# Two full transpositions in place of eight 64x64 products, for the per-head decays of a state-space layer

## The reference, cut to what matters

```
dt = softplus(dt + dt_bias)                # B, L, 64 heads
dA = exp(dt * (-exp(A_log)))
state = state * dA + (dt * x_t) B_t        # at each token, per head
y_t = state . C_t
```

## Time and profile before

| | |
|---|---|
| median of three runs | 776.09 us (773.34 to 778.7) |
| span of the profiled execution | 779.8 us |
| TensorE busy | 742.3 us (95%) |
| VectorE, ScalarE, GpSimd busy | 520.5, 492.4, 293.4 us |
| mean granted TensorE clock | 0.988 of full speed |
| one block in the middle of the mixer | 60 to 61 us |
| all eight-product turns, matmul records | 256, 11.6 us |
| make_dt, make_d, make_cum | 2.3, 2.3, 3.4 us in 8 blocks |
| step_decay, RUN, TO_END | 1.5, 2.4, 4.6 us in 8 blocks |

### The profile page before, as it was taken

The page is one execution under the profiler, slowest core; times in us unless marked ns, Lnnn a source line. Parts: engine busy times, 40 slices in busy tenths (PEclk is TensorE's granted clock), DMA queues, the critical chain, the costliest instruction groups (busy, mean ns, idle before and its releaser), DMA issues.

```text
span 779.8 us, 20312 instructions
## 1 busy us (share of the span) xinstructions
PE 742.3 (95%) x8486; PEld 609.8 (78%) x8486; DVE 520.5 (67%) x845; ACT 492.4 (63%) x933; POOL 293.4 (38%) x235
## 2 busy tenths in 40 slices
PE   4977999999999999999999998889999999999997
PEld 4855788888887887887887886568888888888886
DVE  6968976886887888797797796873633532632331
ACT  5989878978978977978879888533312321321330
POOL 2173275366456546627617707530010011001002
PEclk9988999999999999999999999999999999999999
DMA  9824243384485266266465378634113013003002
GB/s 297 228 69 109 44 105 111 92 241 127 82 236 142 79 158 211 88 148 201 139 158 184 83 202 316 200 99 160 41 55 108 0 37 125 0 13 95 0 1 84
DMA packets 42299, 94.97 MB, mean 122 GB/s; under 512 B 9888, under 2 KB 15776, under 8 KB 42016
## 3 DMA queue, kind: packets, MB, share of 16 engines
q1 hardware_dynamic: 42208, 93.67, 41.9%
HBM read 84.73 MB, written 17.57 MB: 131 GB/s over the span
## 4 chain that ended last, share of the span: by engine, by line
PE 60%; DVE 22%; ACT 10%; issue 5%; DMA 1%; POOL 1%; SPq 0%; DVEq 0%; ACTq 0%; POOLq 0%
PE ps_y L1684 10%; PE ps_proj L1671 9%; DVE cx L937 9%; PE ps_out L1671 6%; PE ps_x L1671 6%; PE ps_proj L1223 4%; PE ps_x L1272 4%; PE ps_proj L1224 3%; PE ps_proj L1225 3%; PE ps_y L1295 3%; DVE ring L992 3%; ACT ring L716 2%; DVE state L1002 2%; PE ps_x L1306 2%; DVE dt_p L912 2%
## 5 line engine op out<-in xcount | busy, mean ns | idle before, releaser
L531 POOL TENSOR_TENSOR ring<-tokd,ring 128x1024 f32<-128x1024 f32 x64 | 122.2, 1924 | 185.2 <-ACT tokd L711 127.5
L1223 PE MATMUL ps_proj<-xn_hi,win_x_hi 128*128 128x256 f32 x352 | 104.7, 298 | 1.7 <-DVE xn_lo L906 1.7
L1224 PE MATMUL ps_proj<-xn_lo,win_x_hi 128*128 128x256 f32 x352 | 100.2, 285 | 0.0
L1225 PE MATMUL ps_proj<-xn_hi,win_x_lo 128*128 128x256 f32 x352 | 100.0, 284 | 0.0
L937 DVE SCALAR_TENSOR_TENSOR cx<-cin,consts,cx 128x256 f32<-128x256 f32 x240 | 96.3, 475 | 0.0
L1540 POOL TENSOR_TENSOR res<-res,hidden 128x512 f32<-128x512 f32 (+1 forms) x16 | 20.1, 1256 | 166.3 <-DVE hidden L1603 165.3
L1223 PEld LDWEIGHTS ps_proj<-xn_hi,win_x_hi 128*128 128x128 f32 x352 | 67.7, 192 | 15.7 <-issue 14.0
L992 DVE TENSOR_TENSOR ring<-ring,ps_tok 128x1024 f32<-128x1024 f32 x64 | 75.6, 1214 | 4.8 <-ACT ring L720 4.7
L1223 PE MATMUL ps_proj<-xn_hi,win_z_hi 128*128 128x256 f32 x256 | 74.0, 289 | 0.0
L1224 PE MATMUL ps_proj<-xn_lo,win_z_hi 128*128 128x256 f32 x256 | 72.2, 282 | 0.0
L1225 PE MATMUL ps_proj<-xn_hi,win_z_lo 128*128 128x256 f32 x256 | 72.1, 282 | 0.0
(11 more groups left out here) (186 smaller groups left out, 1887.3 us busy)
## 6 DMA issues: line engine op xcount, KB each, us to landing
ring<-cum_dram SPq DMA_DIRECT2D x128, 256.0 KB, 4.8
xin<-x SPq DMA_DIRECT2D x8, 512.0 KB, 3.9
res<-x SPq DMA_DIRECT2D x32, 128.0 KB, 2.7
x_dram<-res SPq DMA_DIRECT2D x32, 128.0 KB, 2.9
res<-x_dram SPq DMA_DIRECT2D x16, 256.0 KB, 2.7
out<-res SPq DMA_DIRECT2D x15, 256.0 KB, 2.1
x_in_sb<-x_dram SPq DMA_DIRECT2D x3, 1024.0 KB, 5.6
gate_w_copy<-gate_w SPq DMA_DIRECT2D x4, 704.0 KB, 6.1
```

Source lines behind the costliest of these rows:

```text
L531: pool.tensor_tensor(ring[:, g, :, :], own, ring[:, g, :, :], ALU.subtract).then_inc(diffed, 1)
L1223: pe.matmul(out, hi[:, k, :], xn_hi[:, k, :], start=(k == 0), stop=False)
L1224: pe.matmul(out, hi[:, k, :], xn_lo[:, k, :], start=False, stop=False)
L1225: made = pe.matmul(out, lo[:, k, :], xn_hi[:, k, :], start=False, stop=(k == KT - 1))
```

## The change

`dts` goes. In its place are two tiles, each 128 partitions x 2 steps x 2 sequences x 64 tokens: `dt_cum` has DT of the 64 heads on partitions 0 to 63 (UPPER) and CUM on 64 to 127 (LOWER); `run_end` has RUN on UPPER and TO_END on LOWER. A step's 128 columns of each are turned by one 128x128 transposition. The result in PSUM, and all that reads it, is laid out as before. make_dt becomes two instructions, one a sequence, on 64 partitions each; make_d and the scan become one each on 64 partitions and 256 columns; RUN likewise; TO_END becomes four instructions a block (its bias is a column for one step and one sequence). One wait moves from the scan to make_d (the scan now works in place, so that make_d is the first to overwrite CUM); one wait of ScalarE goes, as dt_p is no longer read by the scan. `low_row`, a small row of the later test on the MLP's weights, moves into `low_buf`, whose readers are done by then.

```diff
-        dts = sb("dts", [P, 4, P])
+        dt_cum, run_end = sb("dt_cum", [P, STEPS, BATCH, Q]), sb("run_end", [P, STEPS, BATCH, Q])
+        UPPER, LOWER = slice(0, HEADS), slice(HEADS, P)
-        chain = sb("chain", [P, P])
+        chain = sb("chain", [P, STEPS * BATCH * Q])
...
-                    sp.dma_start(cum_dram[bass.ds(i, 1), j, :, :].rearrange("a r t -> (a r) t"),
-                                 dts[:, CUM, half(j)]).then_inc(cum_out, 16)
+                    sp.dma_start(cum_dram[i, j, :, :].rearrange("(b h) t -> h b t", b=BATCH),
+                                 dt_cum[LOWER, j, :, :]).then_inc(cum_out, 16)
...
-                    act.wait_ge(cum_made, j)
...
-                act.activation(step_decay[:], dts[:, CUM, Q - 1::Q], ACT.Exp).then_inc(step_decayed, 1)
+                act.activation(step_decay[:].rearrange("h b j -> h j b"), dt_cum[LOWER, :, :, Q - 1], ACT.Exp).then_inc(step_decayed, 1)
                 act.wait_ge(tokd_turned, STEPS * i)
-                act.activation(dts[:, RUN, :], dts[:, CUM, :], ACT.Exp).then_inc(run_made, 1)
+                act.activation(run_end[UPPER, :, :, :], dt_cum[LOWER, :, :, :], ACT.Exp).then_inc(run_made, 1)
                 for j in range(STEPS):
-                    at = (j + 1) * Q - 1
-                    made = act.activation(dts[:, TO_END, half(j)], dts[:, CUM, half(j)], ACT.Exp, scale=-1.0,
-                                          bias=dts[:, CUM, at:at + 1])
+                    for b in range(BATCH):
+                        made = act.activation(run_end[LOWER, j, b, :], dt_cum[LOWER, j, b, :], ACT.Exp, scale=-1.0,
+                                              bias=dt_cum[LOWER, j, b, Q - 1:Q])
...
-                dve.tensor_tensor(dts[:, DT, :], dt_v[:], dt_p[:], ALU.add).then_inc(dt_made, 1)
+                for b in range(BATCH):
+                    r = slice(b * HEADS, (b + 1) * HEADS)
+                    made = dve.tensor_tensor(dt_cum[UPPER, :, b, :], by_step(dt_v, r), by_step(dt_p, r), ALU.add)
+                made.then_inc(dt_made, 1)
...
-                dve.tensor_scalar(dt_p[:], dts[:, DT, :], neg_a[:], LOWEST, ALU.mult, ALU.max).then_inc(d_made, 1)
+                dve.tensor_scalar(dt_cum[LOWER, :, :, :], dt_cum[UPPER, :, :, :], neg_a[UPPER, :], LOWEST, ALU.mult, ALU.max).then_inc(d_made, 1)
...
-                dve.tensor_tensor_scan(dts[:, CUM, :], chain[:], dt_p[:], 0.0, ALU.mult, ALU.add).then_inc(cum_made, 1)
+                cums = dt_cum[LOWER, :, :, :].rearrange("p j b t -> p (j b t)")
+                dve.tensor_tensor_scan(cums, chain[LOWER, :], cums, 0.0, ALU.mult, ALU.add).then_inc(cum_made, 1)
...
-                for n in range(4):
-                    for b in range(BATCH):
-                        made = pe.matmul(ps_tokd[half(b), n * HEADS:(n + 1) * HEADS], dts[half(b), n, half(j)], eye[half(b), half(b)],
-                                         start=True, stop=True)
+                for n, pair in enumerate((dt_cum, run_end)):
+                    made = pe.transpose(ps_tokd[:, n * P:(n + 1) * P], pair[:, j, :, :].rearrange("p b t -> p (b t)"), eye[:])
                 made.then_inc(tokd_turned, 1)
```

More of the change, by code:

```diff
@@ L130, in __init__ @@
         self.low_buf = sb(ctx, "low_buf", [P, LOW_WIDTHS[2]])
-        self.low_row, self.low_any = sb(ctx, "low_row", [1, P]), sb(ctx, "low_any", [1, 1])
+        self.low_row, self.low_any = self.low_buf[0:1, 0:P], sb(ctx, "low_any", [1, 1])
         self.stats, self.moments = sb(ctx, "stats2", [P, TT, 6]), sb(ctx, "moments2", [P, TT, 2])
@@ L181, in mixer_phase @@
         dt_v, dt_e, dt_p = sb("dt_v", [P, P]), sb("dt_e", [P, P]), sb("dt_p", [P, P])
-        dts = sb("dts", [P, 4, P])
+        dt_cum, run_end = sb("dt_cum", [P, STEPS, BATCH, Q]), sb("run_end", [P, STEPS, BATCH, Q])
+        UPPER, LOWER = slice(0, HEADS), slice(HEADS, P)
         tok = sb("tok", [P, P])
         tokd = sb("tokd", [P, STEPS, 4, HEADS])
-        whole, step_decay = sb("whole", [P, BATCH * HEADS, STEPS]), sb("step_decay", [P, STEPS])
+        whole, step_decay = sb("whole", [P, BATCH * HEADS, STEPS]), sb("step_decay", [HEADS, BATCH, STEPS])
         consts = sb("consts", [P, C_N])
@@ L471, in _ @@
             sp.wait_ge(hand.low_all_made, 1)
-            sp.dma_start(hand.low_row[:], hand.low_all[:]).then_inc(hand.low_in, 16)
+            sp.dma_start(hand.low_row, hand.low_all[:]).then_inc(hand.low_in, 16)
             sp.dma_start(hand.scales[:], mlp_packed).then_inc(hand.scales_in, 16)
@@ L912, in soft, with by_step @@
                 dve.scalar_tensor_tensor(dt_p[:], dt_p[:], log_c[LOGN - 1 - n], dt_e[:], ALU.add, ALU.mult).then_inc(soft_step, 1)
+            def by_step(t, r):
+                return t[r, :].rearrange("p (j t) -> p j t", j=STEPS)
             def make_dt(j, opening=False):
@@ L917, in make_dt, with make_d, make_cum @@
                     dve.wait_ge(tokd_turned, STEPS * j)
-                dve.tensor_tensor(dts[:, DT, :], dt_v[:], dt_p[:], ALU.add).then_inc(dt_made, 1)
-            def make_d(j):
+                for b in range(BATCH):
+                    r = slice(b * HEADS, (b + 1) * HEADS)
+                    made = dve.tensor_tensor(dt_cum[UPPER, :, b, :], by_step(dt_v, r), by_step(dt_p, r), ALU.add)
+                made.then_inc(dt_made, 1)
+            def make_d(j, opening=False):
                 dve.wait_ge(dt_made, j + 1)
-                dve.tensor_scalar(dt_p[:], dts[:, DT, :], neg_a[:], LOWEST, ALU.mult, ALU.max).then_inc(d_made, 1)
-            def make_cum(j, opening=False):
-                dve.wait_ge(d_made, j + 1)
                 if not opening:
                     dve.wait_ge(cum_out, 32 * j)
-                dve.tensor_tensor_scan(dts[:, CUM, :], chain[:], dt_p[:], 0.0, ALU.mult, ALU.add).then_inc(cum_made, 1)
+                dve.tensor_scalar(dt_cum[LOWER, :, :, :], dt_cum[UPPER, :, :, :], neg_a[UPPER, :], LOWEST, ALU.mult, ALU.max).then_inc(d_made, 1)
+            def make_cum(j):
+                dve.wait_ge(d_made, j + 1)
+                cums = dt_cum[LOWER, :, :, :].rearrange("p j b t -> p (j b t)")
+                dve.tensor_tensor_scan(cums, chain[LOWER, :], cums, 0.0, ALU.mult, ALU.add).then_inc(cum_made, 1)
             def conv_tap(j, tiles, k):
@@ L1139, in any_low @@
                 dve.wait_ge(hand.low_in, 16)
-                dve.tensor_reduce(hand.low_any[:], hand.low_row[:], mybir.AxisListType.X, ALU.max,
+                dve.tensor_reduce(hand.low_any[:], hand.low_row, mybir.AxisListType.X, ALU.max,
                                   apply_absolute_value=True).then_inc(hand.low_any_made, 1)
@@ L1179, in _ @@
             dve.wait_ge(a_negated, 1)
-            make_d(0)
+            make_d(0, opening=True)
             dve.wait_ge(filled, 2)
-            make_cum(0, opening=True)
+            make_cum(0)
             conv_taps(0, CONV_ORDER[0:2])
```

2 lines of the change are left out of this document (1 added, 1 removed).

## The result

The changed kernel took 783.98 us (median of 6 runs, 781.62 to 791.58), the one before beside it 775.15 (6 runs): ratio 1.013, 95% interval 1.0096 to 1.0163 (the two medians alone make 1.011). The prediction said 777.8, a range of 771.5 to 783.5, and "within 1%" with 0.88. It was wrong: the median lies 0.5 us above the range, and the change cost 8.8 us between the two medians for the 1.7 that the sum had. The sign was right, in part by luck, since a large part of the loss was in no term of the sum.

The account below looks back on a forecast made before the run. TensorE was taken to bound each block's first half and VectorE mainly the second. Opening +0.59, block 0 -0.09, block 1 -0.15, blocks 2, 3, 5, 6 +0.76, block 4 +0.58 sum to +1.7: 777.8 us, range 771.5 to 783.5.

Parts of the forecast that it names:

- Where the path lies: In a block, TensorE holds the chain in the first half, mainly VectorE in the second; the change touches both.
- make_run was covered: ScalarE's make_run, +0.59 us, counts in the opening only; in the blocks 0.5 us of cover hides it.
- Rival A: TensorE bounds both halves and the others' additions are hidden: -5.5 us, 770.6 us; chance 0.12.
- TensorE's turn: Turn of the decays: two transpositions take 0.22 us for 0.61, saving 0.39 a turn, 0.67 in block 0.
- rival B: Two transpositions of a turn do not overlap: saving only 0.06 us, sum +3.9, 780.0 us; chance 0.10.
- VectorE: make_dt +0.23, make_d +0.08, scan +0.26 us: together +0.58 a block (0.36 to 0.87).
- rival C: The additions are at their high ends: +6.1 us, 782.2 us; chance 0.13.
- Opening: Before block 0, ScalarE's longer make_run is on the path: +0.59 us.
- Block 0: -0.67 + 0.58 = -0.09: Block 0: TensorE's turn saves 0.67 us at the lower clock, VectorE's additions cost 0.58.
- line 900's 2126 ns: VectorE's line 900 can be held up fourfold beside GpSimd; at make_d GpSimd is idle, so this does not arise.
- D: Transpositions do not count as work and the clock falls: 15 us in six blocks, 793 us; chance 0.03.
- What the sum was set against: Whole run: profiled span 779.8 us becomes 781.5; the median of runs lies 3.7 below, 776.1 to 777.8.

Follow-up runs that it names:

- less_act: Changed kernel with ScalarE's make_run cut back to its old size from block 1 on, VectorE's steps still long: 784.08 us, 1.0089 to the kernel before.
- rep_after: The changed kernel again, unchanged, on another chip: 784.18 us, ratio 1.0093 to the kernel before.
- cheap_early: Kernel before with two transpositions for eight products in its first two turns only (opening and block 0): 780.43 us, 1.0058.
- ctl_before: The kernel before, unchanged, for more executions and a second trace: 777.01 us, ratio 0.9995.
- cheap_late: Kernel before with two transpositions for eight products in all turns but the first two: 775.58 us, 0.9984.

## Why the prediction was wrong, step by step

- *Where the path lies*: right for blocks 1 to 6. First halves gained by TensorE's term, second halves lost by VectorE's, and make_run was covered (less_act). Rival A (770.6) is out: TensorE did not take xpad up at once.
- *TensorE's turn*: the duration of a transposition was right (272 to 317 ns), and two overlap, so rival B is out. 0.37 on the chain was not 0.22, so by the pieces alone 0.24 is saved. But from the turn's start to the second product of the projection behind it, it is 0.83 us before (179.75 to 180.58) and 0.40 after (120.83 to 121.23), as that projection's first product now starts beside the second transposition. The half block gains 0.4, so the term of 0.39 stands.
- *VectorE*: mis-sized. +0.74 a block for +0.58; the second add near its high end, and the overlap of first tap and scan is gone. Over six blocks that is 6 x 0.16 = 1.0 us. A slip is in the term too: taps of 7.21 us for 18 with a last one of 0.475 are (7.21 - 0.475)/17 = 0.396 us apart, not 0.37, which makes the second add 0.26 and the term 0.61. Here rival C was half right.
- *Opening*: +0.59 is neither shown nor ruled out: ScalarE's table load behind the opening's taps (line 698) starts at 34.5 and 35.1 us in the traces of after, at 34.6 and 34.2 in those of before: 0.4 between the means, with a spread as large within one kernel.
- *The failed step* is "Block 0: -0.67 + 0.58 = -0.09", with the opening's 0.59 before it: +0.5 for the start of block 1, where the traces have +2.6. It was worked out from durations alone, as if the other engines stood still around a turn 0.7 us shorter. What the traces show in its place: VectorE's lines 884 and 900 meet GpSimd's work and last 12.9 and 10.9 us for 9.7, so step 1's xpad comes 2.6 and 1.8 us late; step 1's `carry` at full clock takes 1.7 us off again; VectorE's additions bring 0.74; and in rep_after block 1's first `carry` falls to half clock behind a wait of 1.97 us and costs 1.7. Some 0.4 us in each trace is not named. The prediction looked at line 900's 2126 ns and asked for that collision at make_d only, not where it stood. cheap_early shows about 4 us in the median for those turns without any addition of VectorE's, by a second way that the sum did not have: fewer instructions, a stall for them, and half clock behind it.
- *The clock* (D): it did fall, but not by the transpositions; in blocks 1 to 6 once in each trace of after, behind waits of 1.98 and 1.97 us for xpad. D's chance of 0.03 was for the wrong mechanism. Its price, 2.5 us for 10 us at 0.75, took granted clock for time on the path; a `carry` at half clock costs up to 1.7 us there, and for the 10 us at 0.75 in block 0 themselves no cost is shown.
- *What the sum was set against*: from block 7's first `scale_carry` to the end the four traces take 301.1 (before), 299.0 (ctl_before), 295.8 (after) and 301.1 us (rep_after). The difference is mostly block 7's first half, 27.0 and 25.2 us before, 21.8 and 23.3 after: the traces of before have their wait for instructions there, 2.7 and 2.0 us, those of after do not. Behind it, it is 274.1 and 273.8 before, 274.0 and 277.8 after. So the two profiled spans, 0.5 us apart, hid a loss that the blocks show.
- *Adding up*: the start of block 1 +2.6, blocks 1 to 6 +3.2, make 5.8 of the 7 to 10 us that the two ratios give. Block 7's first half takes 3.6 back in these traces and the rest adds 2.0, which makes the 4.2 us by which the means of the two spans of each kernel differ. The medians differ by more, since both profiled executions of before (781.6 and 778.1 us) ran above its medians (775.2 to 777); what a typical execution of before does in block 7 is in no trace, and this rest stays open. The stores out of 64 partitions (their issue on SyncE takes 632 ns for 385; the rows of `ring` land in 5.6 us for 4.7 in ctl_before) may be in it.

## What to carry to other kernels

When two engines hold the path in turn, an edit that moves work from one to the other gains at one half and pays at the other; price the receiving side as a sequence in its place (no overlap at the end, each small instruction in full), not by columns. Read the start of a kernel separately from its steady blocks, and ask of each event there that comes earlier which SBUF-heavy instruction of VectorE it will now lie beside. A test that puts one resource right (the clock in block 0) and gains nothing does not yet show that nothing waited for it: look in its trace whether the gain is there and something else has moved.

## What was not expected of the hardware

- TensorE's instructions arrive in pieces of 16 KB (67, 66 or 65 in a run). With 56 of some 20,300 instructions taken out of the first 60 us (20,256 left) the trace has a stall of 3.2 us beside such a piece, and the granted clock is 0.50 for the 5 us behind it; with 56 fillers in their place it has neither. In the traces looked at the stall stands where q1 alone keeps the 16 DMA engines busy. It is not in every execution: of two traces of the changed kernel one has it.
- One `carry` of eight products takes 1.94 us at full clock and 3.63 at half, and which it is at the same place of the same code differs between executions (3.63 in before and ctl_before, 1.94 in cheap_late, at step 1 of block 0).
- Halving the partitions from 128 to 64 did not shorten an add: 293 ns became 286.
- With 44 transpositions more in block 0 the mean granted clock of the kernel before rose from 0.989 (34 executions) to 0.993 (12): in this kernel, transpositions count as work for the clock. The stretch of 50 to 60 us alone would not show it, as rep_after has 1.00 there without any filler.
